# A gated cross-attention block with a mixture of experts on one Trainium2 core: moved tiles, whole-row operands, first products by blocks, and part of the rounding on ScalarE

## What is computed

```python
# first half: quantised product with the context, one scale per 128-block
xq = quant_dequant_act_1x128(layernorm(x))        # fp8 values, scale per token and block
wq = quant_dequant_weight_128x128(ctx_2048)       # fp8 values, scale per 128x128 block
x  = x + tanh(g_xattn[0]) * einsum("emk,enk->emn", xq, wq)

# second half: mixture of 8 experts (top 4) and one shared expert
h = layernorm(x)
probs = softmax(h @ gate_w.T); top_w, top_i = top_k(probs, 4); top_w /= top_w.sum(-1)
g = einsum("th,eih->eti", h, wg); u = einsum("th,eih->eti", h, wu)
y = einsum("eti,ehi->eth", silu(g) * u, wd)
moe = einsum("te,eth->th", comb, y)               # comb holds top_w at top_i
sh  = silu(h @ swg.T) * (h @ swu.T) @ swd.T
x = x + tanh(g_ffn[0]) * (moe + sigmoid(h @ shared_gate_w.T) * sh)
```

## Time and profile before

| | |
|---|---|
| median of 3 runs | 189.81 us (189.59 to 190.03) |
| profiled execution, device time | 189.74 us |
| its span, first to last instruction | 187.9 us |
| PE busy | 162.2 us, 86% |
| DVE busy | 130.6 us, 69% |
| ACT busy | 101.3 us, 54% |
| POOL busy | 77.8 us, 41% |
| mean granted TensorE clock | 0.997 |

### The profile page before, as it was taken

One profiled execution on the slowest core, in us unless ns is written; L12 is line 12 of the kernel. 1 busy time (PEld: TensorE's weight loads), 2 busy tenths in 40 slices (PEclk: granted clock), 3 DMA queues, 4 the chain that ended last, 5 costly groups with the idle time before them and its releaser, 6 DMA issues.

```text
span 187.9 us, 2355 instructions
## 1 busy us (share of the span) xinstructions
PE 162.2 (86%) x714; PEld 123.6 (66%) x715; DVE 130.6 (69%) x280; ACT 101.3 (54%) x217; POOL 77.8 (41%) x90
## 2 busy tenths in 40 slices
PE   0023298999999999999999999999999999999992
PEld 0011144787886687667788878878768888888870
DVE  0799996384878999999988845862478545554553
ACT  2449333278777885546665553595553455445430
POOL 3220325044865454443465433444444654544410
PEclk9999999999999999999999999999999999999998
DMA  4599700000289995222332332502999100000003
GB/s 135 178 405 400 307 2 0 0 3 2 64 228 234 326 400 178 85 58 84 84 87 84 84 84 85 195 5 62 230 240 329 67 2 0 0 0 0 0 0 115
DMA packets 11057, 22.75 MB, mean 121 GB/s; under 512 B 1938, under 2 KB 2194, under 8 KB 11044
## 3 DMA queue, kind: packets, MB, share of 16 engines
q1 hardware_dynamic: 10612, 21.94, 37.9%
q10 hardware_dynamic: 432, 0.66, 1.3%
HBM read 21.51 MB, written 1.09 MB: 120 GB/s over the span
## 4 chain that ended last, share of the span: by engine, by line
PE 73%; DVE 16%; issue 3%; DMA 3%; ACT 1%; POOL 1%; DVEq 1%; ACTq 0%; POOLq 0%
PE bank L988 47%; PE bank L1077 6%; PE bank L1078 6%; PE bank L1081 6%; DMA cw<-ctx_t 3%; DVE bank L760 1%; DVE deq_x L660 1%; PE bank L969 1%; DVE x L677 1%; DVE xq L653 1%; DVE silu L745 1%; PE bank L1017 1%; DVE xc L652 1%; POOL rstd L281 1%; DVE amax_c L570 1%
## 5 line engine op out<-in xcount | busy, mean ns | idle before, releaser
L287 POOL TENSOR_TENSOR w_lo<-w_raw,w_hi 128x512 fp32r<-128x512 f32 (+1 forms) x34 | 42.8, 1258 | 61.4 <-ACT w_hi L416 60.6
L988 PE MATMUL bank<-h_hi,w_hi 128*128 128x512 f32 x132 | 53.8, 408 | 0.7 <-DVE bank L756 0.4
L988 PE MATMUL bank<-h_lo,w_hi 128*128 128x512 f32 x132 | 52.2, 395 | 0.0
L988 PE MATMUL bank<-h_hi,w_lo 128*128 128x512 f32 x132 | 52.1, 395 | 0.0
L437 ACT ACTIVATE a_hi<-bank 128x512 fp32r<-128x512 f32 (+1 forms) x34 | 20.3, 598 | 38.7 <-DVE bank L760 38.1
L293 POOL TENSOR_TENSOR w_lo<-w_raw,w_hi 128x256 fp32r<-128x256 f32 (+1 forms) x34 | 26.0, 765 | 19.5 <-ACT w_hi L420 19.4
L760 DVE TENSOR_TENSOR bank<-silu,bank 128x512 f32<-128x512 f32 x32 | 22.2, 695 | 15.1 <-PE bank L988 13.2
L988 PEld LDWEIGHTS bank<-h_hi,w_hi 128*128 128x128 f32 x132 | 24.8, 188 | 8.2 <-issue 3.1
L769 DVE TENSOR_TENSOR a_lo<-bank,a_hi 128x512 fp32r<-128x512 f32 x32 | 22.1, 689 | 11.5 <-ACT a_hi L437 11.3
L988 PEld LDWEIGHTS bank<-h_hi,w_lo 128*128 128x128 f32 x132 | 24.8, 188 | 6.0
L988 PEld LDWEIGHTS bank<-h_lo,w_hi 128*128 128x128 f32 x132 | 24.8, 188 | 4.9
(11 more groups left out here) (108 smaller groups left out, 173.6 us busy)
## 6 DMA issues: line engine op xcount, KB each, us to landing
w_raw<-w_full SPq DMA_DIRECT2D x32, 384.0 KB, 7.4
mix_b<-rows_dram SPq DMA_DIRECT2D x8, 256.0 KB, 6.5
out_t<-fin SPq DMA_DIRECT2D x4, 256.0 KB, 2.1
mix_b<-rows_dram SPq DMA_DIRECT2D x4, 224.0 KB, 6.2
x<-xs SPq DMA_DIRECT2D x3, 256.0 KB, 7.2
mix_b<-rows_dram SPq DMA_DIRECT2D x4, 192.0 KB, 5.9
mix_b<-rows_dram SPq DMA_DIRECT2D x4, 160.0 KB, 5.9
cw<-ctx_t ACTq DMA_DIRECT2D x2, 256.0 KB, 5.5
```

The costliest lines, as they stand in the source:

```text
L287: nc.gpsimd.tensor_tensor(w_lo[:, n % 2, 0:cols], w_raw[:, n % RING, 0:cols], w_hi[:, n % 2, 0:cols].bitcast(F32), ALU.subtract).then_inc( ...
L988: last = nc.tensor.matmul(out, w[k][a], x_of[k][b], start=(start and k == 0 and i == 0), stop=(stop and k == blocks - 1 and i == 2))
```

## The change

1. **Aligned tiles.** `mix_b` to `fin` are named before the small tiles. All of them now begin at a multiple of 64 bytes.
2. **Whole rows.** The short unit's `down` uses all 128 rows of `w_lo`, and POOL makes all 128. `blk_w` and `lg_rows` have 128 rows. The logits (all 128 rows of the bank) are transposed as they are; `fold` is gone, and DVE adds low to high in one more instruction.
3. **The short unit's gate** goes to the unit's UP bank. The unit after it waits no longer for the short unit's `gated`.
4. **First products by blocks.** `transpose_y2_by_blocks`, `high_h_by_blocks` and `low_h_by_blocks` treat batch 1 in two blocks of features; `first_products` takes the high passes of router and gate 0 a block at a time, before any low part. The logits' transposes stand within `up(0)`.
5. **Rounding.** For x of batch 0 and the context of batch 1 ScalarE makes the magic number by a Relu with a bias (`magic`), less `LEAST`, and DVE adds and subtracts with two scalar_tensor_tensor instructions (`rounded`).
6. **Order.** POOL's `low_gate_w` waits no longer for the second xq, `low_gu(0)` waits for the context of batch 1. In `down` the third pass of OUT[0] stands before the second of OUT[1]. x and contexts of batches 0 and 1 come in eight transfers, four on each queue. Four more `keep_clock_up` products stand before `attend(1)`. `transpose_xq(3)`, `attend(2)`, `copy_xqt(3)` and `residual0(2)` stand later.

```diff
+LEAST = SUBNORMAL * MAGIC
...
-            sp.dma_start(x[:, 0:1, :], xs[:, 0:1, :]).then_inc(x_landed[0], 16)
-            load_x(1)
+            for b in range(HB):
+                sp.dma_start(x[:, BT * b:BT * b + 1, :], xs[:, BT * b:BT * b + 1, :]).then_inc(x_landed[b], 16)
+                sp.dma_start(cw[:, b, 0], ctx_t[:, b, 0]).then_inc(ctx_landed[b], 16)
...
-                rows, at = (LAST, GUL) if n % UNITS == SHORT else (P, GU)
+                at = GUL if n % UNITS == SHORT else GU
...
-            pool.wait_ge(xq_ready, 2)
             low_gate_w()
+            pool.wait_ge(cq_ready[1], 1)
             low_gu(0)
...
+            def magic(power, needs):
+
+                a.wait_ge(needs, 1)
+                a.wait_ge(least_filled, 1)
+                nc.scalar.activation(power, power, ACT.Relu, bias=least[:], scale=MAGIC).then_inc(magic_done, 1)
...
+            def high_h_by_blocks(b):
+                ts = slice(b * S, (b + 1) * S)
+                for k, done in enumerate((h_hi_first, h_hi_done)):
+                    a.wait_ge(y2t_psum, KC * b + k + 1)
+                    nc.scalar.activation(h_hi[:, k, ts], Y2T1[k][:, 0:S], ACT.Copy).then_inc(done, 1)
...
+            def rounded(out, val, power, done):
+
+                after(did(nc.vector.scalar_tensor_tensor(val, power, LEAST, val, ALU.add, ALU.add)))
+                nc.vector.scalar_tensor_tensor(out, val, LEAST, power, ALU.subtract, ALU.subtract).then_inc(done, 1)
...
-            exp_x0 = exponents_x(0)
+            exponents_x(0)
             block_max_ctx(0)
-            mag_x0 = magic_x(0, exp_x0)
             scales_x(1, max_x(1))
             scales_ctx(0)
-            round_x(0, mag_x0)
+            v.wait_ge(magic_done, 1)
...
-            exp_c1 = exponents_ctx(1)
+            exponents_ctx(1)
             dequant_scales(0)
-            mag_c1 = magic_ctx(1, exp_c1)
-            round_ctx(1, mag_c1)
+            v.wait_ge(magic_done, 2)
...
+            def first_products():
+
+                pe.wait_ge(gate_split, 1)
+                pe.wait_ge(gu_lo_done, 1)
+                pe.wait_ge(x1t_copied, 2)
+                pe.wait_ge(h_hi_done, 1)
+                pe.wait_ge(h_hi_first, 1)
+                w = w_gu(0, 0)
+                for k in range(KC):
+                    if k == 1:
+                        pe.wait_ge(h_hi_done, 2)
+                    nc.tensor.matmul(LOGIT[0][:], gate_hl[:, k, :], h_hi[:, k, 0:HN], start=(k == 0), stop=False)
+                    nc.tensor.matmul(GATE[:], w[k][0], h_hi[:, k, 0:HN], start=(k == 0), stop=False)
+                    nc.tensor.matmul(GATE[:], w[k][1], h_hi[:, k, 0:HN], start=False, stop=False)
+                pe.wait_ge(h_lo_done, HB)
...
-                    last = nc.tensor.matmul(LOGIT_T[h][:, jj * GP:(jj + 1) * GP], lg_rows[:, jj * P:(jj + 1) * P], fold[:],
-                                            start=True, stop=True)
+                    last = nc.tensor.transpose(LOGIT_T[h][:, jj * P:(jj + 1) * P], lg_rows[:, jj * P:(jj + 1) * P], eye[:])
...
-                if n >= 1:
+                if i == SHORT:
+                    pe.wait_ge(a_lo_done, n - 1)
+                elif n >= 1:
                     was = (n - 1) % UNITS
                     if was < SHORT:
                         pe.wait_ge(silu_done, n)
-                    elif was == SHORT:
-                        pe.wait_ge(act_done, n)
-                    else:
+                    elif was > SHORT:
                         pe.wait_ge(mixed_done, mixes(n - 1))
...
-                        nc.tensor.matmul(OUT[k][:], w_lo[0:LAST, n % 2, cols[k]], a_hi[0:LAST, n % 2, :],
-                                         start=False, stop=stop).then_inc(out_done, 1)
+                        nc.tensor.matmul(OUT[k][:], w_lo[:, n % 2, cols[k]], a_hi[:, n % 2, :], start=False, stop=stop)\
+                            .then_inc(out_done, 1)
```

More of the change, by code:

```diff
@@ L68, in flamingo_gated_block @@
         h_lo = sb("h_lo", [P, KC, T], F32R)
+        mix_b = sb("mix_b", [P, MOE, HN])
+        sg_b = sb("sg_b", [P, HN])
+        w_raw = sb("w_raw", [P, RING, WC])
+        w_hi = sb("w_hi", [P, 2, WC], F32R)
+        w_lo = sb("w_lo", [P, 2, WC], F32R)
+        silu = sb("silu", [P, 2, HN])
+        a_hi = sb("a_hi", [P, 2, HN], F32R)
+        a_lo = sb("a_lo", [P, 2, HN], F32R)
+        fin = sb("fin", [P, 2, HN])
         bn = sb("bn", [P, 2, TILES, 6])
@@ L640, in exponents_x @@
                 flat = "p j k c -> p (j k c)"
-                return did(exponents(xe[:, tile_slice(b)].rearrange(flat), xc[:, tile_slice(b)].rearrange(flat)))
+                last = exponents(xe[:, tile_slice(b)].rearrange(flat), xc[:, tile_slice(b)].rearrange(flat))
+                if b == 0:
+                    last.then_inc(power_x, 1)
+                    return None
+                return did(last)
             def magic_x(b, exponents_step):
@@ L704, in low_h, with low_h_by_blocks @@
                                         h_hi[:, :, ts].bitcast(F32), ALU.subtract).then_inc(h_lo_done, 1)
+            def low_h_by_blocks(b):
+                ts = slice(b * S, (b + 1) * S)
+                v.wait_ge(h_hi_first, 1)
+                nc.vector.tensor_tensor(h_lo[:, 0, ts], Y2T1[0][:, 0:S], h_hi[:, 0, ts].bitcast(F32), ALU.subtract)
+                v.wait_ge(h_hi_done, b + 1)
+                nc.vector.tensor_tensor(h_lo[:, 1, ts], Y2T1[1][:, 0:S], h_hi[:, 1, ts].bitcast(F32), ALU.subtract)\
+                    .then_inc(h_lo_done, 1)
             def route_compare(h):
                 v.wait_ge(logits_t, h + 1)
-                nc.vector.tensor_copy(lg[:], LOGIT_T[h][:, 0:HT * GP].rearrange("p (j g) -> p j g", j=HT)).then_inc(lg_ready, 1)
+                parts = LOGIT_T[h][:].rearrange("p (j r) -> p j r", j=HT)
+                after(did(nc.vector.tensor_copy(lg_low[:], parts[:, :, GP:2 * GP])))
+                nc.vector.tensor_tensor(lg[:], parts[:, :, 0:GP], lg_low[:], ALU.add).then_inc(lg_ready, 1)
                 v.wait_ge(lg_ready, h + 1)
@@ L982, in transpose_y2, with transpose_y2_by_blocks @@
                 transpose_tokens(b, y2, Y2T, y2t_psum)
+            def transpose_y2_by_blocks(b):
+                pe.wait_ge(y2_ready, b + 1)
+                pe.wait_ge(x1t_copied, 1)
+                for k in range(KC):
+                    for jj, j in enumerate(tiles(b)):
+                        last = nc.tensor.transpose(Y2T1[k][:, jj * P:(jj + 1) * P], y2[:, j, k * P:(k + 1) * P], eye[:])
+                    last.then_inc(y2t_psum, 1)
             def three_passes(out, w, x_of, start, stop):
@@ L994, in tokens, with w_gu @@
                 return [(h_hi[:, k, ts], h_lo[:, k, ts]) for k in range(KC)]
+            def w_gu(n, which):
+                at = which * KC * P
+                return [(w_hi[:, n % 2, at + k * P:at + (k + 1) * P], w_lo[:, n % 2, at + k * P:at + (k + 1) * P])
+                        for k in range(KC)]
             def router(h):
[L998 removed]
                 pe.wait_ge(h_hi_done, HB * (h + 1))
[L1000 to L1003 removed]
+                pe.wait_ge(h_lo_done, HB * h + 1)
                 ts = slice(h * HN, (h + 1) * HN)
@@ L1010, in router @@
                 last.then_inc(logits_ready, 1)
+            def first_products():
[5 more added lines that the diff above has]
+                w = w_gu(0, 0)
+                for k in range(KC):
+                    if k == 1:
[4 more added lines that the diff above has]
+                pe.wait_ge(h_lo_done, HB)
+                for k in range(KC):
+                    last = nc.tensor.matmul(LOGIT[0][:], gate_hl[:, k, :], h_lo[:, k, 0:HN], start=False, stop=(k == KC - 1))
+                last.then_inc(logits_ready, 1)
+                for k in range(KC):
+                    last = nc.tensor.matmul(GATE[:], w[k][0], h_lo[:, k, 0:HN], start=False, stop=(k == KC - 1))
+                last.then_inc(gate_done, 1)
             def transpose_logits(h):
@@ L1025, in transpose_comb @@
                 last.then_inc(comb_psum, 1)
-            def w_gu(n, which):
-                at = which * KC * P
-                return [(w_hi[:, n % 2, at + k * P:at + (k + 1) * P], w_lo[:, n % 2, at + k * P:at + (k + 1) * P])
-                        for k in range(KC)]
             def keep_clock_up(count):
@@ L1115, in _ @@
             ctx_block_max(1)
-            gate(6)
-            up(6)
+            unit(6)
             ctx_spread_max(1)
-            down(5)
             unit(7)
@@ L1125, in _ @@
             down(8)
-            gate(10)
+            unit(10)
             transpose_xq(3)
-            up(10)
-            down(9)
             gate(11)
+            up(11)
             attend(2)
-            up(11)
             down(10)
```

111 lines of the change are left out of this document (58 added, 53 removed).

## The result

The changed kernel takes **185.16 us** in the median of 4 runs (184.78 to 185.92), beside 189.80 for the kernel before on the same chip: a ratio of 0.976, 95% interval 0.972 to 0.980. The profiled execution took 185.45 us with a span of 183.0; before it was 189.74 and 187.9. The forecast was 185.8. The total is right, but two terms that it sets at nothing were 1.7 and 1.1 us, with opposite signs. The spans of the four executions are 183.0, 183.0, 183.0 and 183.1 us, and what lies outside the instructions varies from 1.8 to 2.9; so small differences are read from the spans here.

A forecast was written before the change was run, and what follows sets the result against it. DVE was taken to bound the start and units 6 to 12, TensorE the part from 91.5 us on. Terms 1.45 + 0.4 + 0.5 + 0 + 0.65 + 0.7 + 0.2 = 3.9 off 189.74 gave 185.8 us, range 181.5 to 187.4.

The forecast's parts named there:

- A: Start on DVE: earlier context, magic numbers on ScalarE and POOL's moved instruction save 1.45 us in sum.
- (c): Start, context of batch 1: short scale instructions and ScalarE's magic number save 1.25 us from exponents to first addition.
- (d): Start on DVE: four instructions change from tensor_tensor to scalar_tensor_tensor, 0.25 us lost.
- (e): Start: POOL's moved instruction holds up DVE's residual sum, 0.3 us lost.
- B: First product: it waits for a smaller ScalarE copy behind two transposes, no longer four; 0.4 us saved.
- C: First product to gate(3): TensorE's list shrinks, but gate(3) waits for silu(2); 0.5 us saved.
- D: Units 6 to 12: DVE leads and its list keeps its length, so TensorE's savings give 0 us.
- the slower rival: Units 6 to 12: earlier weight work stretches DVE's SBUF-only passes, 0.6 us in each of seven units; 190.1 us, chance 0.06.
- E: Second logits' transposes, where DVE is free: 0.65 us saved.
- F: Short unit of the second half: closer products, limited by gate(25) waiting for mixed(24); 0.7 us saved.
- G: The end: OUT[0] is complete earlier, so the first of DVE's last two instructions starts earlier; 0.2 us saved.
- Aligned tiles: rival at 0.20: All fp32r products, where TensorE leads: alignment makes each cheaper, 3.7 us (7.5 if fully), 182.1 us; chance 0.20.

The follow-up runs named there:

- e10: The changed kernel with the edits of e9, but three of ScalarE's four new passes put behind the silu and weight copy of their unit: 182.16 us.
- e1: The kernel before with one edit, the big tiles moved ahead of the small ones, so that they begin at a multiple of 64 bytes: 189.86 us.
- e3: The changed kernel with only the split weights (both parts) shifted 32 bytes past a multiple of 64: 187.41 us.
- e2: The changed kernel with 32 bytes of padding ahead of and behind the big tiles, which puts them 32 bytes past a multiple of 64: 187.29 us.
- e13: The changed kernel with 64-row operands again for the short unit's low product and the logits' transposes (with the folding matrix): 186.05 us.
- e11: The changed kernel with the scales of batches 2 and 3 on VectorE moved out of the way of GpSimd's w_lo in units 5 and 6: 185.44 us.
- e9: The changed kernel with ScalarE also making the magic numbers of batches 2 and 3, and one shared-part addition moved to unit 16: 185.09 us.

## Why the prediction was right in sum

The measured 185.16 us lie in the stated range of 181.5 to 187.4 and 0.6 below the forecast; part of that is luck, as the terms show. The range of the forecast alone, 184.5 to 187.2, is not the sum of its terms' bounds: added up they give 183.3 to 188.4.

*A, start on VectorE, 1.45 forecast, 1.79 measured.* (a) The context: from VectorE's first instruction to the maxima of x 2.35 us for 2.77, 0.42 (0.4 forecast). (b) From there to the first rounding 5.58 for 5.89, 0.31 (0.35). (c) Exponents to first addition 1.21 for 2.40, 1.19 (1.25). (d) The fused instruction with three operands takes 0.68 and 0.69, no longer than the plain one: so nothing is lost, where I subtracted 0.25 by the price of a row whose scalar comes from a tile (0.75). (e) 0.13, where I took 0.3. The Trainium skill, page "SBUF — State Buffer", section "Who interferes with whom", calls the shared port pair an exclusive lock; by it VectorE's sum would stand still for the whole overlap, 0.27 us here. Its length shows 0.13, so the trace agrees in kind and not in size.

*B, first product, 0.4 and 0.40.* From the first residual to the first product 8.73 us for 9.00, 0.27, and the 0.13 of (e) lie in it.

*C, to gate(3), 0.5 and 0.64.* 13.29 for 13.93 us. gate(3) starts 0.14 after silu(2) as it waits for it, so 0.22 of this are slack of TensorE that went, and VectorE behind it gets no more than 0.42.

*D, units 3 to 12: 0 forecast, 1.14 lost.* This step failed. Its mechanism held in units 6 to 12: VectorE leads there, as e10 shows, and gate(n) waits for mixed(n-1) from gate(7) on, which starts 0.14 us after mixed(6) ends. The price of nothing failed. I wrote "Even the time that DVE loses to POOL stays, since POOL and ScalarE follow DVE there", but this holds only where VectorE leads; in units 3 to 5 silu waits for TensorE's products, and the split of the weights on ScalarE and GpSimd stands behind it. That work came earlier against VectorE and fell onto two of its instructions, 0.54 and 0.44 us. Alignment alone is enough for that (e1), and so is the rest of the change with the weights out of alignment (e3). Of these 0.98 some 0.34 filled idle time of VectorE. With the 0.22 of slack from C and 0.28 more in units 6 to 12 (a pass of 0.43 that now takes 0.85, less what the scales behind it gain) it is 1.14. That is the mechanism of the slower rival, which asked for 0.6 in each of seven units; it got 0.28 in all seven, and the larger part came in units 4 and 5, where no rival looked for it.

*E, F, G, 1.55 forecast, about 1.2 measured.* Between gate(13) and the last product 2.69 are gained; 1.66 are alignment (e2), 1.03 are left, of which e13 gives 0.50 to the rows. The other 0.5 wasn't taken apart; the new order of the down products is in it. Each piece has the forecast size on TensorE (0.67 for the transposes, 0.70 in the short unit), but mixed(24) takes more of it than I wrote: TensorE now waits for it where TensorE itself was late. G, from the start of the last product on, gave 0.13 (3.97 for 4.10).

*Aligned tiles: rival at 0.20, half true.* I set the effect at nothing in the forecast, on the argument that `h_hi` was aligned, `a_hi` was not, and both kinds stood at even distances. It was wrong because the weights were off in both kinds, and one operand is enough. Nor did the distance come to the filler's 0.217, so that of the 7.5 us priced in the rival some 1.7 are there.

The sum of the profiled spans: chance at the first instruction 0.4, A 1.79, B 0.40, C 0.64, D -1.14, gate(13) to the last product 2.69, end 0.13, together 4.9 (187.9 to 183.0). Two errors, 1.7 and 1.1 us, cancelled in part; that the total came out is luck to this extent. With the alignment alone undone the changed kernel takes 187.3 to 187.4 us (e2, e3), some 1.5 above the forecast, since the loss in D stays.

## What to carry to other kernels

A gain on the leading engine moves everything that follows it, also an engine whose work holds up the next leader: ask where the follower's instructions will land, not only how long the leader gets. Two leads of about 0.2 us, from different parts of the change, each cost some 1 us in this way, so undoing the one part (e3) did not bring the time back. Take work off the engine that leads before you move single instructions out of a collision, since here the collision came back at the next one (e11), while one pass less was a gain with its collision (e10). And put nothing with a far wait ahead of the instruction that the next engine needs: the same edits gave next to nothing in e9 and 3 us in e10.
